# Four stages of a transformer kernel: projections at other steps, fewer unread products, plain down products, folded weights

## The chip, the cores and the metric

The kernel runs on one core of a Trainium2 chip. The time is the device time of one execution in microseconds (us). The engines are TensorE (PE), VectorE (DVE), ScalarE (ACT), GpSimd (POOL) and SyncE (SP, which issues DMAs). PEclk is the clock that TensorE was granted, 1.0 being 2.4 GHz and 0.5 being 1.2 GHz.

## The reference

A sequence batch `x` (64 sequences, 128 tokens, 128 channels) goes through four layers. Layer 0 is window self-attention, top-k cross-attention and a gated MLP. Layers 1 and 2 are each a modulated self-attention with 16 heads of 8 channels, a cross-attention to 77 context rows and a GELU MLP (128 to 512 to 128). Layer 3 ("refine") is a cross-attention with one head to the raw context, whose result goes with the normalised tokens into a router, three experts and a gate. All is float32. What matters here:

```python
# layers 1 and 2, self (cross: q from x, k and v from the context)
x_norm = modulate(_ln(x), shift_a, scale_a)
q, k, v = split(x_norm @ W_qkv + b_qkv)              # 16 heads of 8
x = x + gate_a * (softmax(q @ k.T * scale) @ v @ W_proj + b_proj)
# their MLP
h = gelu(x_norm2 @ W_mlp1 + b_mlp1)
x = x + gate_m * (h @ W_mlp2 + b_mlp2)               # the down product
# layer 3
q, k, v = nx @ Wq, prototype_bank @ Wk, prototype_bank @ Wv
evidence = softmax(q @ k.T * H ** -0.5) @ v
combined = concat([nx, evidence, anchor])            # to router_W, e_w1, gate_w1
```

## The kernel before

The tokens stay in SBUF as `x_res` from the first stage to the last. Work is cut into 16 groups of four sequences (512 tokens). The stages follow one another: setup, window attention, top-k attention, MLP of layer 0 (to 1409 us), attention of layer 1 (to about 2098), its MLP (to 2248), attention of layer 2 (to about 2929), its MLP (to 3084), refine (to the end).

**Attention of layers 1 and 2** (`packed_attention_layer`) takes 32 groups through one pipeline, first 16 of self-attention, then 16 of cross-attention. A group is eight steps, u = 0 to 7 (of half a sequence's heads each). The order on every engine is written out by hand in the `body` functions, and what is done of which group at which step stands in constants:

- At each step PE multiplies queries by keys (`attn_s`, L1616, eight 32-row products), DVE takes row maxima of it (L1491, two), the negated maxima go by ACT (`attn_om`, L1367) and a DMA of POOL back into the packed queries, and seven steps later (LT) PE makes the transposed scores (`attn_t`, L1631), ACT the exponentials (`attn_pT`, L1374, two a step), PE the products with the values (L1656). `s_ps`, the PSUM bank pair of the scores, is single: PE's next scores wait for DVE's maxima, and DVE's next maxima for the scores.
- Two groups ahead, PE transposes the normalised tokens at step XT (L1584), makes keys at KP (L1592), queries at QP (L1597) and values at VP (L1604), all into the one bank `l_ps`. So keys wait until ACT has modulated `attn_hT`; queries until ACT and then DVE have read the keys out of the bank, as a high part (`attn_kT`, L1349) and a low part (L1466); values until the same was done with the queries (`attn_qT`, L1355 and L1471). These are four steps of one chain through PE, ACT and DVE.
- Keys and queries are then packed by DMA (SP: 12 of keys, L1267; 12 of queries, L1253; 2 of zero rows, L1255, a group). SP starts a group's keys when DVE has made their low part and PE has made the last transposed scores of the group before (`s_st`, reached at step 6). ACT's `queries_out` (L1355) waits for the DMAs of the group before, which read the same `attn_qT`.
- The output of a group takes one projection (PROJ, L1756), ACT's `attn_pg` (L1388 to L1392), and is added to `x_res` (L1527).
- `keep_clock` (L1676) issues products that nobody reads, 128x512 each, UNREAD[u] of them at step u, to keep PE busy. They stand behind the step's scores and write `l_ps`.

**The MLPs of layers 1 and 2** (`mlp_layer`) make up and down products as three fp32r products each (`product3`, L238 to L240) from high and low parts, which stand for one fp32 product. The high part of the GELU output `mlp_hid` is a cast of DVE (L1943, four a group), the low part a subtraction of POOL (L1870, three a group) or DVE (L1949, one).

**Refine** takes 16 groups. Per group PE makes keys (L2486), queries (L2491) and values (L2496, eight records), ACT reads out keys (L2385) and queries (L2389), DVE the values (L2246); then scores, softmax, evidence, router, experts.

## Time and profile before

| | |
|---|---|
| median of 3 runs | 3493.57 us (3489.97 to 3500.9) |
| the profiled execution | 3496.01 us, span 3494.2 us |
| PE busy | 3048.8 us, 87% of the span |
| PE weight loads | 2051.7 us |
| DVE | 2754.6 us, 79% |
| ACT | 2253.2 us, 64% |
| POOL | 1170.7 us, 34% |
| PEclk over the run | 0.947 |

The engines' shares are means over stages of different kinds, and none is at 100%, so the stage is what has to be read. Unread products count as busy time of PE. In a row of a timeline the first number is the start in us from the start of the span, the second the busy time of one or more like instructions (xcount); in brackets stands how long the engine had been idle before and what ended the wait.

### The profile page before, as it was taken

The page shows a single profiled execution, that of the slowest core. Times are in us where ns is not written, and L with a number is a line of the kernel's source. Part 1 is how long each engine was busy: PE and PEld are TensorE (multiplying, and loading weights), DVE is VectorE, ACT ScalarE, POOL GpSimd, SP SyncE. Part 2 cuts the span into 40 slices and gives each one's busy share as a digit, 9 for nine tenths or more (in the row PEclk, how much of TensorE's full clock was granted, in tenths as well). Part 3 has the DMA queues.
Part 4 walks back from the last instruction along what each step waited for, and adds up shares of the span by engine and source line. Part 5 has one row for each costly group of instructions (what it writes and reads, how often), then busy time and mean ns, then how long its engine had stood idle before and what let it go on. Part 6 is the DMA issues. An engine that isn't in the chain of part 4 may idle for free. (4 is left out here: it accounts for less than half of the span.)

```text
span 3494.2 us, 94730 instructions
## 1 busy us (share of the span) xinstructions
PE 3048.8 (87%) x32127; PEld 2051.7 (59%) x32127; DVE 2754.6 (79%) x12477; ACT 2253.2 (64%) x5572; POOL 1170.7 (34%) x1374
## 2 busy tenths in 40 slices
PE   6999967777777779799999997789999997879999
PEld 3444434444444457566666665556666665568887
DVE  4878779999999978588877759778887776946665
ACT  2666667777777667377766665457776665646665
POOL 0000046666666656311122215521112212532111
PEclk9999979999899889799999999989999999979999
DMA  1111000000000000244444420034444440000000
GB/s 47 44 49 37 14 12 7 9 9 9 8 9 7 3 1 1 72 106 107 107 103 100 104 60 1 20 97 108 106 107 101 105 100 17 1 24 13 11 12 16
DMA packets 139908, 162.90 MB, mean 47 GB/s; under 512 B 41318, under 2 KB 88870, under 8 KB 139174
## 3 DMA queue, kind: packets, MB, share of 16 engines
q1 hardware_dynamic: 127270, 130.80, 14.9%
q0 software_dynamic: 12160, 26.04, 3.2%
q8 instruction: 262, 4.29, 0.5%
q14 instruction: 216, 1.77, 0.2%
HBM read 16.33 MB, written 4.19 MB: 6 GB/s over the span
## 5 line engine op out<-in xcount | busy, mean ns | idle before, releaser
L1374 ACT ACTIVATE attn_pT<-attn_t 128x512 f32<-128x512 f32 (+1 forms) x1024 | 555.7, 597 | 319.7 <-PE attn_t L1631 319.5
L1491 DVE TENSOR_REDUCE attn_mx<-attn_s 128x4 f32<-128x512 f32 (+1 forms) x1024 | 549.4, 578 | 140.2 <-PE attn_s L1616 139.1
L1616 PEld LDWEIGHTS attn_s<-packed_keys,packed_queries 32*128 32x128 f32 x4096 | 276.7, 189 | 161.5 <-DVE attn_mx L1491 96.0
L659 ACT ACTIVATE topk_prob<-topk_s,topk_nmx 128x77 f32<-128x77 f32 x1024 | 248.3, 326 | 181.7 <-DVE topk_work L840 156.0
L1289 POOL DMA_DIRECT2D packed_queries<-attn_om x256 | 142.7, 557 | 645.0 <-ACT attn_om L1367 640.9
L1616 PE MATMUL attn_s<-packed_keys,packed_queries 32*128 32x128 f32 (+1 forms) x4096 | 341.5, 287 | 13.3 <-DVE attn_mx L1491 7.2
L503 POOL TENSOR_SCALAR topk_mask<-topk_work 128x308 f32<-128x308 f32 x256 | 250.1, 977 | 238.9 <-DVE topk_work L845 237.8
L1023 PE MATMUL topk_s<-kbd,topk_qT 128*128 128x308 f32 x512 | 215.4, 505 | 129.7 <-ACT topk_prob L659 129.2
L1656 PE MATMUL attn_o<-attn_pT,attn_vp 128*18 128x128 f32 (+1 forms) x8192 | 326.3, 277 | 0.0
L1631 PE MATMUL attn_t<-packed_queries,packed_keys 32*128 32x128 f32 (+1 forms) x4096 | 299.8, 264 | 0.0
L1870 POOL TENSOR_TENSOR mlp_hid<-mlp_hid 128x512 fp32r<-128x512 f32 x160 | 210.1, 1314 | 156.8 <-DVE mlp_hid L1943 107.9
L1631 PEld LDWEIGHTS attn_t<-packed_queries,packed_keys 32*128 32x128 f32 (+1 forms) x4096 | 227.4, 166 | 4.7 <-ACT attn_pT L1374 3.4
L1676 PE MATMUL attn_l<-packed_keys 128*128 128x512 f32 x636 | 225.2, 444 | 0.7 <-DVE attn_vp L1481 0.7
L507 POOL TENSOR_TENSOR topk_prob<-topk_prob,topk_mask 128x308 f32<-128x308 f32 x256 | 213.8, 835 | 21.3
L840 DVE MATCH_REPLACE8 topk_work<-topk_top,topk_s 128x77 f32<-128x77 f32 x1024 | 220.2, 223 | 0.0
L1656 PEld LDWEIGHTS attn_o<-attn_pT,attn_vp 128*18 128x18 f32 (+1 forms) x8192 | 181.3, 97 | 60.6 <-issue 44.4
L845 DVE MATCH_REPLACE8 topk_work<-topk_top,topk_work 128x77 f32<-128x77 f32 x1024 | 215.3, 219 | 0.0
L1023 PEld LDWEIGHTS topk_s<-kbd,topk_qT 128*128 128x128 f32 x512 | 86.6, 210 | 195.5 <-ACT topk_prob L659 141.4
L1033 PEld LDWEIGHTS topk_t<-ident,topk_prob 128*77 128x77 f32 x1024 | 146.5, 163 | 58.2 <-issue 16.5
L829 DVE MAX8 topk_top<-topk_s 128x8 f32<-128x77 f32 x1024 | 167.0, 222 | 15.4 <-PE topk_s L1023 15.0
L1033 PE MATMUL topk_t<-ident,topk_prob 128*77 128x128 f32 x1024 | 170.4, 294 | 1.8 <-POOL topk_prob L507 1.8
L1285 POOL TENSOR_TENSOR attn_rstd<-attn_vareps,neg_half 128x4 f32<-128x4 f32 x64 | 65.8, 1029 | 299.9 <-DVE attn_vareps L1449 299.8
(316 smaller groups left out, 7869.7 us busy)
## 6 DMA issues: line engine op xcount, KB each, us to landing
packed_queries<-attn_qT SPq DMA_DIRECT2D x720, 64.0 KB, 2.2
packed_keys<-attn_kT SPq DMA_DIRECT2D x384, 64.0 KB, 2.1
packed_queries<-attn_om POOLq DMA_DIRECT2D x256, 64.0 KB, 2.3
packed_queries<-zero_rows SPq DMA_DIRECT2D x120, 128.0 KB, 2.7
packed_keys<-attn_kT SPq DMA_DIRECT2D x384, 39.0 KB, 2.2
kbd<-window_kT SPq DMA_DIRECT2D x512, 8.0 KB
kbd<-topk_kT SPq DMA_DIRECT2D x512, 4.8 KB
x_res<-in_x SPq DMA_DIRECT2D x16, 192.0 KB, 2.6
```

The lines of the kernel that those rows point to most:

```text
L503: nc.gpsimd.tensor_scalar(mask[:, u % 2, :], work[:, n % NP, :], NEG / 2, None, ALU.is_le).then_inc(s_mask, 1)
L659: last = nc.scalar.activation(prob[:, n % NP, h * keys:(h + 1) * keys], s_ps[:, u % 2, h * keys:(h + 1) * keys], ACT.Exp, scale=SCALE, bia ...
L840: last = nc.vector.match_replace(wk_[now][:, h, :], top[:, u % 2, h, :], sc[:, h, :], NEG)
L845: last = nc.vector.match_replace(wk_[past][:, h, :], top2[:, c % 2, h, :], wk_[past][:, h, :], NEG)
L1023: last = nc.tensor.matmul(s_ps[:, u % 2, 0:cols], qT[:, par, b * T:(b + 1) * T], r.kbd[:, HU * g:HU * g + HU, b * keys:(b + 1) * keys], st ...
L1033: last = nc.tensor.transpose(t_ps[0:rows, c % 2, j * T:(j + 1) * T], prob[:, n % NP, j * rows:(j + 1) * rows], r.ident[:, :])
L1374: nc.scalar.activation(pT[0:keys, c % 2, h, :], t_ps[0:keys, h, :], ACT.Exp, scale=SCALE).then_inc(s_exp, 1)
L1491: nc.vector.tensor_reduce(mx[:, (c // 2) % 2, 2 * k + h, :], sc, AX.X, ALU.max).then_inc(s_max, 1)
L1616: last = nc.tensor.matmul(s_ps[:, h, k * KW:(k + 1) * KW], r.qp[32 * j:32 * j + 32, buf, k, b * T:(b + 1) * T], r.kp[32 * j:32 * j + 32, b ...
L1631: last = nc.tensor.matmul(t_ps[0:keys, h, k * T:(k + 1) * T], r.kp[32 * j:32 * j + 32, buf, k, b * KW:b * KW + keys], r.qp[32 * j:32 * j + ...
L1656: last = nc.tensor.matmul(o_ps[32 * k:32 * k + 18, v * T:(v + 1) * T], vp[0:keys, buf, b, k, v, a, :], pT[0:keys, c % 2, a, k * T:(k + 1) ...
L1676: nc.tensor.matmul(l_ps[:, :], r.kp[:, buf, 0, 0:T], r.kp[:, buf, 0, :], start=True, stop=True)
```

## The change

1. In the attention of layers 1 and 2, XT, KP, QP and VP are 1, 3, 5 and 7 in place of 3, 5, 6 and 7, and the normalisation of the group that comes three later is spread over steps 0, 2, 4 and 6. The unread products are five a group in place of nine, and `keep_clock` stands ahead of the step's scores, behind the wait for the maxima, and writes the scores' bank.
2. In the MLPs of layers 1 and 2 the down product is one plain fp32 product of `hid` and the weights as they are. The casts, the subtractions and the split of the down weights are gone.
3. In refine, a prologue makes `wqk` = Wq times Wk transposed and multiplies Wv into the rows of the experts', the gate's and the router's weights that take the evidence. So the raw context serves as keys and as values: the values are loaded for each group by a DMA of SP into one of three buffers, and the key and value projections and their copies are gone.

```diff
-    XT, KP, QP, VP = 3, 5, 6, 7
+    XT, KP, QP, VP = 1, 3, 5, 7
-    UNREAD = (2, 3, 2, 2)
+    UNREAD = (2, 1, 1, 0, 0, 0, 1, 0)
...
@@ DVE, body
                     if there(before, left, 3):
+                        if u == 0:
+                            ln_stats(i + 3, (0, 1))
                         if u == 2:
-                            ln_stats(i + 3, (0, 1, 2))
-                        if u == 3:
-                            ln_stats(i + 3, (3,))
+                            ln_stats(i + 3, (2, 3))
                             ln_variance(i + 3)
-                        if u == XT + 1:
+                        if u == 4:
                             ln_apply(i + 3, (0, 1))
-                    if u == 0 and i > 0 and there(before, left, 2):
-                        ln_apply(i + 2, (2, 3))
+                        if u == 6:
+                            ln_apply(i + 3, (2, 3))
...
@@ PE
-            def keep_clock(g, buf, count):
-                pe.wait_ge(s_v, min(g + 2, NT))
+            def keep_clock(buf, count):
                 for _ in range(count):
-                    nc.tensor.matmul(l_ps[:, :], r.kp[:, buf, 0, 0:T], r.kp[:, buf, 0, :], start=True, stop=True)
+                    nc.tensor.matmul(s_ps[:, 0, :], r.kp[:, buf, 0, 0:T], r.kp[:, buf, 0, :], start=True, stop=True)
...
                     if now:
                         scores_waits(i, u)
+                        keep_clock(m3, UNREAD[u] if there(before, left, 2) else 2)
...
-                    if now and u < len(UNREAD):
-                        keep_clock(i, m3, UNREAD[u])
...
@@ mlp_layer: DVE loses L1943 and L1949, POOL L1870; PE
+                if not swiglu:
+                    pe.wait_ge(s_hid, n + 1)
+                    nc.tensor.matmul(y_ps[:, par, :], r.W(name, c * C), hid[:, c % NB, :],
+                                     start=(c == 0), stop=(c == NC - 1)).then_inc(s_down, 1)
+                    return
...
@@ refine
+            def load_values(g):
+                sp.dma_start(v[:, g % 3], r.ctx_v[:, G * g:G * g + G, :]).then_inc(s_vin[g % 3], 16)
...
+            nc.tensor.matmul(t_ps[:, 0:C], r.W("q3"), r.W("k3"), start=True, stop=True).then_inc(s_qkps, 1)
...
+                for e in range(E):
+                    out = t_ps[:, e * RH:(e + 1) * RH] if e < 2 else u_ps[:, 1, 2 * C:2 * C + RH]
+                    nc.tensor.matmul(out, r.W("v3"), r.W("e1", (e * 3 + 1) * RH, RH), start=True, stop=True)
+                nc.tensor.matmul(g_ps[:, B * E:B * E + C], r.W("v3"), r.W("g1", C), start=True, stop=True)
+                nc.tensor.matmul(g_ps[:, B * E + C:B * E + C + E], r.W("v3"), r.W("rw", E, E), start=True, stop=True)
...
-                nc.tensor.matmul(l_ps[:, :], r.W("q3"), nx[:, g % NXB, :], start=True, stop=True).then_inc(s_qps, 1)
+                nc.tensor.matmul(l_ps[:, :], wqk[:, :], nx[:, g % NXB, :], start=True, stop=True).then_inc(s_qps, 1)
```

How ACT's work of one self group of layer 1 stands in a row from step 5 on, before (`attn_kT` are the keys, `attn_qT` the queries of two groups ahead, `attn_pT` the exponentials, two a step):

```order
L1374 ACTIVATE attn_pT<-attn_t 128x512 x2
L1349 ACTIVATE attn_kT<-attn_l,bias_cols 128x512
L1392 ACTIVATE attn_pg<-attn_f,gate_bias,mod 128x128
L1367 COPY attn_om<-attn_o 128x384
L1374 ACTIVATE attn_pT<-attn_t 128x512 x2
L1355 ACTIVATE attn_qT<-attn_l,bias_cols 128x512
L1374 ACTIVATE attn_pT<-attn_t 128x512 x2
L1392 ACTIVATE attn_pg<-attn_f,gate_bias,mod 128x128 x3
```

The same engine from step 3 on, now:

```order
L1349 ACTIVATE attn_kT<-attn_l,bias_cols 128x512
L1367 COPY attn_om<-attn_o 128x384
L1374 ACTIVATE attn_pT<-attn_t 128x512 x4
L1355 ACTIVATE attn_qT<-attn_l,bias_cols 128x512
L1392 ACTIVATE attn_pg<-attn_f,gate_bias,mod 128x128
L1367 COPY attn_om<-attn_o 128x384
L1374 ACTIVATE attn_pT<-attn_t 128x512 x4
L1392 ACTIVATE attn_pg<-attn_f,gate_bias,mod 128x128 x3
```

The queries were read out at step 6, behind that step's `attn_pg`, `attn_om` and exponentials; now they stand at step 5 ahead of all of these, and of step 7's exponentials.

PE between the scores of steps 0 and 1, before:

```order
L1681 MATMUL attn_f<-ident,attn_pg 128x128 x4
L1676 MATMUL attn_l<-packed_keys 128x512 x2
L1667 MATMUL attn_r<-ident,attn_om 128x128 x2
L1656 MATMUL attn_o<-attn_pT,attn_vp 18x128 x8
L1616 MATMUL attn_s<-packed_keys,packed_queries 128x128
```

PE at the same place now:

```order
L1680 MATMUL attn_f<-ident,attn_pg 128x128 x4
L1667 MATMUL attn_r<-ident,attn_om 128x128 x2
L1656 MATMUL attn_o<-attn_pT,attn_vp 18x128 x8
L1675 MATMUL attn_s<-packed_keys 128x512
L1616 MATMUL attn_s<-packed_keys,packed_queries 128x128
```

The unread product has moved from a place that needs no maxima to the place between the wait for them and the scores (L1616).

## Rows read from the trace of the kernel before

The columns of a window are its stretch and length, the busy time and the count of instructions of PE, PEld (weight loads), DVE, ACT and POOL (of PE alone in rows 2 and 11, of L1616 and L2008 alone), the granted clock of PE, the busy share of the DMA engines and GB/s.

**Rows 1.** Busy time by engine in three stretches: attention 1, MLP 1, refine.
```profile
1500.00:1750.00 250.00, 234.30 (x3749) 157.96 (x3741) 219.27 (x666) 183.36 (x383) 41.22 (x64) 1.00 0.43 106
2125.00:2225.00 100.00, 82.86 (x378) 59.60 (x377) 92.98 (x248) 64.85 (x141) 58.18 (x47) 1.00 0.00 1
3150.00:3475.00 325.00, 325.00 (x2116) 283.30 (x2115) 205.65 (x615) 200.05 (x542) 66.78 (x54) 1.00 0.05 12
```
**Rows 2.** Windows: scores (L1616) of 11 self groups, 13 cross groups, one cross group.
```profile
1505.45:1728.32 222.87, 58.42 (x705) 1.00 0.44 107
1787.35:2039.08 251.73, 66.90 (x832) 0.99 0.42 103
1963.21:1982.05 18.84, 5.12 (x64) 1.00 0.44 106
```
**Rows 3.** Timeline of PE in one self group of layer 1.
```profile
1568.16 0.32 PE L1616 MATMUL attn_s<-packed_keys,packed_queries 32*128 32x128 f32 x1
1569.36 0.94 PE L1676 MATMUL attn_l<-packed_keys 128*128 128x512 f32 x3
1570.27 0.32 PE L1616 MATMUL attn_s<-packed_keys,packed_queries 32*128 32x128 f32 x1
1577.64 0.32 PE L1616 MATMUL attn_s<-packed_keys,packed_queries 32*128 32x128 f32 x1
1578.92 1.02 PE L1592 MATMUL attn_l<-attn_hT,weights 128*128 128x512 f32 x2
1579.88 0.32 PE L1616 MATMUL attn_s<-packed_keys,packed_queries 32*128 32x128 f32 x1
1581.59 1.13 PE L1597 MATMUL attn_l<-attn_hT,weights 128*128 128x512 f32 x2 [1.05 <-DVE attn_kT L1466]
1585.76 0.29 PE L1616 MATMUL attn_s<-packed_keys,packed_queries 32*128 32x128 f32 x1
```
**Rows 4.** Timeline of DVE in that group, row maxima.
```profile
1568.92 1.29 DVE L1491 TENSOR_REDUCE attn_mx<-attn_s 128x4 f32<-128x512 f32 x2 [0.40 <-PE attn_s L1616]
1581.53 1.28 DVE L1491 TENSOR_REDUCE attn_mx<-attn_s 128x4 f32<-128x512 f32 x2
1584.23 1.28 DVE L1491 TENSOR_REDUCE attn_mx<-attn_s 128x4 f32<-128x512 f32 x2
```
**Rows 5.** Timeline of ACT in that group, the queries' copy.
```profile
1582.84 0.69 ACT L1355 ACTIVATE attn_qT<-attn_l,bias_cols 128x512 fp32r<-128x512 f32 x1 [0.38 <-PE attn_l L1597]
```
**Rows 6.** Timeline of SP: one group's first keys and last zero rows.
```profile
1561.49 8.98 SPq L1267 DMA_DIRECT2D packed_keys<-attn_kT  x12
1579.75 0.64 SPq L1255 DMA_DIRECT2D packed_queries<-zero_rows  x1
```
**Rows 7.** DMA issues of the page: KB each, us from issue to landing.
```profile
packed_queries<-zero_rows SPq DMA_DIRECT2D x120, 128.0 KB, 2.7
```
**Rows 8.** What ACT waited for, 1800 to 2050 us.
```profile
ACT attn_qT L1355 <- DMA packed_queries<-zero_rows: 4.6, 6, 1.4
```
**Rows 9.** Windows of layer 2, before and at a fall of the clock.
```profile
2658.00:2661.40 3.40, 1.52 (x24) 1.12 (x23) 1.58 (x4) 2.02 (x4) 0.00 (x0) 1.00 0.36 93
2661.40:2665.00 3.60, 3.60 (x27) 2.72 (x25) 2.84 (x11) 1.07 (x2) 1.29 (x2) 0.53 0.50 121
```
**Rows 10.** What PE waited for, whole run: us in total, times, longest.
```profile
PE mlp_l L2008 <- DVE mlp_xn L1895: 56.4, 32, 6.3
PE attn_l L1597 <- DVE attn_kT L1466: 54.1, 64, 3.6
```
**Rows 11.** Window of eight MLP groups, their transposes (L2008), four a group.
```profile
2168.05:2237.15 69.10, 5.02 (x32) 1.00 0.00 1
```
**Rows 12.** Timeline of PE in MLP 1: a down product's first record, what follows it.
```profile
2177.90 0.39 PE L238 MATMUL mlp_y<-mlp_hid,mlp_w 128*128 128x512 f32 x1
2178.60 0.60 PE L2048 MATMUL mlp_r<-ident,mlp_pg 128*128 128x128 f32 x4
```
**Rows 13.** Timeline of PE in refine: one group's values.
```profile
3256.66 1.04 PE L2496 MATMUL refine_l<-weights,ctxT 128*77 128x128 f32 x8
```

More of the change, by code:

```diff
@@ L1716, in body @@
                         scores_waits(i, u)
+                        keep_clock(m3, UNREAD[u] if there(before, left, 2) else 2)
+                    elif back:
+                        after(pe, s_max, 2 * NS * NT)
+                        keep_clock((m3 + dg) % 3, 2)
                     if back:
@@ L1731, in body @@
                         rows_of_projection(i - 3)
-                    if now and u < len(UNREAD):
-                        keep_clock(i, m3, UNREAD[u])
-                    elif not there(before, left, 2) and (now or back):
-                        keep_clock(i, m3, 2)
                     if there(before, left, 2):
@@ L1990, in body @@
                     if work and not swiglu:
-                        after(act, s_lo, n - 3)
+                        after(act, s_down, n - 3)
                         act.wait_ge(s_up, n + 1)
@@ L2150, in _ @@
                          ).then_inc(s_rows, 16)
+            for g in range(3):
+                load_values(g)
             for g in range(NG):
                 p = g % 2
+                if there(g + 3):
+                    sp.wait_ge(s_eps, g + 1)
+                    load_values(g + 3)
                 sp.wait_ge(s_y, g + 1)
@@ L2304, in prepared @@
                 nc.vector.tensor_copy(arb[:, :, :], by_batch(g_ps[:, 0:B * E], E)).then_inc(s_arb, 1)
+                for k, (product, parts) in enumerate(folded()):
+                    dve.wait_ge(s_fhi, k + 1)
+                    nc.vector.tensor_tensor(parts[1], product, parts[0].bitcast(F32), ALU.subtract).then_inc(s_flo, 1)
             def gate_bias(g):
@@ L2426, in prepare @@
                 act.wait_ge(s_w3, 16)
[L2427 to L2430 removed]
+                nc.scalar.copy(up_part(0, 0), e1_first).then_inc(s_w1hi, 1)
+                nc.scalar.copy(w1s[:, 0, E * 2 * RH:E * 2 * RH + C], r.W("g1", 0, C)).then_inc(s_w1hi, 1)
             def prepared():
@@ L2438, in prepared @@
                                          ).then_inc(s_w2ow, 1)
+                for k, (product, parts) in enumerate(folded()):
+                    if k == 2:
+                        act.wait_ge(s_arb, 1)
+                        nc.scalar.copy(wr[:, :], g_ps[:, B * E + C:B * E + C + E]).then_inc(s_wr, 1)
+                    nc.scalar.copy(parts[0], product).then_inc(s_fhi, 1)
+            act.wait_ge(s_qkps, 1)
+            nc.scalar.copy(wqk[:, :], t_ps[:, 0:C]).then_inc(s_wqk, 1)
             for i in range(-2, NG):
@@ L2455, in _ @@
                     hidden(i, 3)
-                if new:
-                    keys_out(i + 2)
                 if now:
@@ L2477, in transpose_xn @@
             def transpose_xn(g):
-                after(pe, s_v, g)
+                after(pe, s_qT, g)
                 pe.wait_ge(s_xn, g + 1)
@@ L2614, in _ @@
                     router(i + 1)
-                if new:
-                    project_keys(i + 2)
                 if now:
@@ L2622, in _ @@
                     up(i, 5)
-                if new:
-                    project_values(i + 2)
                 if now:
```

93 lines of the change are left out of this document (41 added, 52 removed).

## The prediction

> **What bounds the kernel now.** I read the page's busy shares first, then windows by stage, because the shares of the whole run mix stages, then the timeline of one group engine by engine, and last the lists of waits. In attention no engine is full: PE is busy 234 of 250 us, but with unread products in that, DVE 219, ACT 183 [rows 1]. What sets the pace is a ring: scores on PE, maxima on DVE, and the next scores. With T for the start of a step's scores and M for its maxima, M comes 0.76 us after T (1568.16 to 1568.92) and the next T 1.35 us after M (1570.27) [rows 3, 4]. Eight such steps would take 17 us; a self group takes 222.87/11 = 20.26 us, a cross group 251.73/13 = 19.36 us [rows 2]. The rest comes from the steps with projections and from DVE's other work. The MLPs are bound by DVE (93 of 100 us, PE 83), refine by PE (325 of 325) [rows 1].
>
> **Attention: a self group step by step.** What the change takes away is the wait of PE's queries for the keys' low part: 64 times, 54.1 us in all [rows 10]. In the group shown it is 1.05 us at 1581.59 [rows 3]. It also removes four of nine unread products; three take 0.91 us from the first to the next scores (1569.36 to 1570.27), so 0.30 each [rows 3]. What it adds: the five that stay stand between the wait for the maxima and the scores, so each of them is on the ring, where the nine stood in gaps. And keys and queries no longer share one stall.
>
> I rebuild a group. T0 is the moment that the maxima of step 7 are done.
> - Steps 0 to 2: two unread products (0.60) and 0.76 to M0; then 1.35 + 0.30 + 0.76 = 2.41 to M1; to M2 the same 2.41, or a little more by DVE, which has in step 1 the maxima (1.29), a normalisation and the addition to x, for which I add 0.03; then 1.35 to T3. Sum 7.56 us.
> - Steps 3 and 4: the keys are projected 1.28 us after T (1577.64 to 1578.92), and their low part comes in front of the next maxima, which start at T + 3.89 (1581.53) [rows 3, 4]. Behind it 1.35: 5.24 us from T3 to T5.
> - Steps 5 and 6: the queries likewise 1.28 after T, the maxima behind their low part 2.64 after that (1581.59 to 1584.23) [rows 3, 4], and one more negation of about 0.08 by my estimate: T + 4.00, + 1.35: 5.35 us from T5 to T7. The unread product of step 6 is covered by this stall.
> - Step 7: 0.76 to M7, and 1.53 from M7 to the next group (1584.23 to 1585.76), which the values' projection sets [rows 3, 4]: 2.29 us.
>
> That is 20.44 us, against 20.26 us on average before [rows 2]. Two stalls of 3.9 and 4.0 us apart cost more than the pair in a row before, and the ring carries 1.2 us of unread products of which the change took no visible time away in the gaps. So the 54.1 us of the removed wait are not won; they turn into DVE waiting at steps 4 and 6.
>
> **The DMAs behind it.** The queries' copy on ACT waits for the DMAs of the group before. SP works from a group's first keys (1561.49) to its last zero rows (1579.75) for 18.26 us, and these land 2.7 us after issue: 20.96 us from the first keys to the landing [rows 6, 7]. Before, the copy that needs it stood at 1582.84, 21.35 us after 1561.49, so 0.4 us to spare [rows 5, 6]; in cross groups, which are shorter, ACT waited there in 6 of about 13, up to 1.4 us [rows 8]. Now the copy stands at step 5, at T5 + 1.28 + 1.25 = T5 + 2.53 (1.25 from 1581.59 to 1582.84 [rows 3, 5]). The keys' DMAs do not start earlier, though the keys are ready two steps sooner: they also wait for the last transposed scores of step 6, about 0.7 us after T6, and T6 is T5 + 0.76 + 1.65 = T5 + 2.41. So the room is the group's length G less (2.41 + 0.7 - 2.53) = G - 0.58, where it was G + 1.28. A late copy by s lengthens the group, and so the room, by s: s = 20.96 + 0.58 - 20.44 - s gives s = 0.55. Self group: 21.0 us, +0.7 on 20.26, times 32: +24 us. What hangs on ACT behind the late copy: `attn_pg`, `attn_om` and the exponentials of steps 6 and 7, for which PE's values and next transposed scores wait.
>
> Cross groups: the one of 18.84 us has no wait for DMAs [rows 2]. By the same steps it becomes about 18.3 (bounds 17.8, if all four removed products and a part of the stall are won, and 18.84, if nothing is). Then s = (20.96 + 0.58 - 18.3)/2 = 1.6: 19.9 us. The rule gives before (20.96 - 1.28 - 18.84)/2 = 0.4, so 19.26 where 19.36 is measured, and I add that 0.1: 20.0, +0.65 on 19.36, times 32: +21 us. Bounds for both kinds together: if landing never binds, self 20.44 and cross 18.3, +6 - 34 = -28 us; if SP's spacing is that of its slower groups, some 21.7 us to the landing, +24 + 21 + 64 x 0.37 = +69.
>
> **The clock.** With fewer unread products and a stall of 1.6 us a cross group PE is idle more. At 2661.4 the granted clock is 0.53 (the 1.2 GHz level) for 3.6 us, and before it PE had been busy for only 1.52 of 3.4 us [rows 9]. Such a fall costs about half its length, 1.7 us. There are four of them in the attention before, all in cross groups; a window of cross groups has 0.99, one of self groups 1.00 [rows 2]. I take 12 more, +20 us; bounds 0 and one in each of 64 groups, +109. The Trainium skill ("TensorE: Matmul & The Clock Gate", section "A second HAM failure mode: psum-queue depth-cycling") says that a PE which is idle in many short bits between groups of matmuls swings between its two clocks. Rows 9 agree that it falls after such a stretch; by that rule most groups would see a fall, which is the slower rival below.
>
> **MLPs.** A group takes 69.10/8 = 8.64 us [rows 11], PE busy 83% [rows 1], so 7.16 us, of which I take 6.8 for work, since records overhang the next ones. DVE loses four casts and a subtraction and is then far from the bound. PE becomes it: the plain fp32 product takes 0.96 us to the next scores (1578.92 to 1579.88) [rows 3], three fp32r products 0.70 (2177.90 to 2178.60) [rows 12]. I keep 0.85 as the lower end, in case the product's start overlaps more here. Four a group add 0.6 to 1.0 to 6.8: 7.6 us. Of 8.64 that saves 1.04, times 16 groups, times 2 layers: -33 us, and 1 for the split in the prologue: -34 (bounds -27, PE at 7.8, and -41). PE's wait for `mlp_xn`, 56.4 us [rows 10], is what it eats into.
>
> **Refine** is PE-bound, so what leaves PE is won: the values (1.04 with the last record's overhang, about 0.8 of PE's time) [rows 13] and the keys (308 of 512 columns of a plain product of 0.96: 0.58) [rows 3]: 1.4 us, times 14 full groups: -20 us. The new prologue puts about eight fp32 products, three copies and three subtractions ahead of the first expert product, partly while the weights' DMA is awaited: +3. Net -17 (bounds -22 and -10). The values' DMAs, 16 of them on SP, which is idle there, are hidden.
>
> **Sum.** +24 + 21 + 20 - 34 - 17 = +14 us on the execution profiled, 3496.0, gives 3510; the median of the runs shown is 3493.6, 2.4 lower: 3508 us.
>
> **Rivals.**
> - A (this forecast, 0.43): DMA landing binds at step 5. 3508, its own range 3480 to 3540.
> - B (0.12), the stall really goes: queries find their keys ready, four products are won in full. Self falls by 54.1/64 = 0.85 and about 0.3 of unread products to 19.1, cross to 18.2: -37 - 37 - 34 - 17 = -125 us, 3369. For it: the wait stands in the list [rows 10]. Against: the chain from projection to DVE's low part is as long at a step of its own.
> - D (0.20), SP and landing do not bind (the DMAs issue faster when they are not behind the keys, or the copy finds them landed): self 20.44, cross 18.3, clock little: -28 - 34 - 17 + 5 = -74 us, 3420. For it: only 6 of 13 cross groups wait today [rows 8].
> - C (0.25), slower: the granted clock falls to 0.5 in most groups, since the wait at step 5 empties PE just where the unread products were taken out. It decides once a stretch like 2658 to 2661.4 comes in every group: half of the groups at 1.7 us, +54, all of them +109, in place of my 20: 3540 to 3600. Against it: three of four steps keep PE near full, and a self group has 20 us of work a group that is 90% busy.
> That the change does not do what it says has no rival here: the order of the engines shows the moves.
>
> **How the numbers follow.** The range, 3425 to 3555, takes in D and the lower half of C and leaves out B and the far end of C, about 2 in 10. No change is within 0.3%, 3483 to 3504, which is about what a measurement of this kernel can tell. A gives slower in 0.25 of its 0.43, same in 0.13, faster in 0.05; C slower, 0.22, with 0.03 same; B and D faster, 0.30, with 0.02 same. So faster 0.35, same 0.18, slower 0.47.
>
> **What would show it.** After the change, ACT's queries' copy waits for the zero rows' DMA in most groups, 0.5 us in self and 1.5 in cross groups; the projection of queries never waits for the keys' low part; self groups take 21.0 and cross groups 20.0 us; maxima at steps 4 and 6 wait for low parts. Each unread product lies right before scores. MLP groups at 7.6 us with PE full; refine's period 1.4 us shorter. Wrong it is if copies do not wait for DMAs (D), if the steps 3 and 5 take 2.3 us (B), or if PEclk shows dips in most groups (C).

## The result, and the profile after

The changed kernel takes 3591.61 us in the median of 4 runs (3560.1 to 3649.82), against 3493.21 us before (3489.97 to 3500.9): the ratio is 1.025 (1.0248), 95% interval 1.017 to 1.033. It is slower, outside of the range on record. The ratios, here and below, leave out runs more than 1.5% above the quickest of their kernel (here 3649.82 us, at a granted clock of 0.894), while the us given are medians of all runs. The execution profiled is the quickest, 3560.1 us with a mean granted clock of 0.926; the two others took 3579 us at 0.915 and 3604 us at 0.910.

From the page of the changed kernel, the span, the busy times and the clock by slices:

```profile
span 3558.3 us, 93096 instructions
PE 3065.5 (86%) x31607; PEld 2017.6 (57%) x31607; DVE 2623.0 (74%) x12300; ACT 2243.9 (63%) x5561; POOL 1044.2 (29%) x1278
...
PEclk9999989999899799899998898989999797989999
```

The busy shares hide the change: PE is at 86%, before at 87%. The stages do, each from PE's first instruction in it to the first of the next: attention 1 went from 691.6 to 750.2 us, attention 2 from 691.0 to 767.6, the two MLPs from 146.1 and 150.2 to 123.7 and 123.7, refine from 405.1 to 384.5. So +135 in attention, -49 in the MLPs, -21 in refine, and 1.6 less before them: 64 us, the difference of the spans.

Windows with the scores alone (L1616), 12 self and 12 cross groups of layer 1, then of layer 2; the columns after the length are PE's busy time in these products, their count, the granted clock, the DMA share and GB/s:

```profile
1509.45:1765.75 256.30, 63.78 (x768) 0.98 0.40 99
1830.45:2089.35 258.90, 64.82 (x768) 0.89 0.38 93
2380.33:2635.14 254.81, 63.73 (x768) 0.98 0.41 101
2703.80:2967.99 264.19, 68.23 (x768) 0.87 0.37 90
```

That is 21.36 and 21.23 us a self group, 21.57 and 22.02 a cross group, where it was 20.26 and 19.36 [rows 2]. The clock is 0.98 in self and 0.89 and 0.87 in cross groups. In the trace's records of the clock there are 33 falls to 0.5 from each layer's group 3 to its group 29 (of 32, counted from 0), 26 of them in cross groups; before there were 4. Together they last 201 us, before 14.

What PE waited for, whole run (us, times, longest), and ACT's copy of the queries:

```profile
PE attn_r L1667 <- ACT attn_om L1367: 95.1, 64, 4.6
PE attn_s L1616 <- DVE attn_mx L1491: 33.8, 67, 1.9
PE mlp_l L2001 <- DVE mlp_xn L1896: 17.9, 4, 6.3
```

```profile
ACT attn_qT L1355 <- DMA packed_queries<-zero_rows: 64.9, 35, 4.4
```

The wait of the queries' projection for the keys' low part, 54.1 us [rows 10], is gone. In its place stands 95.1 us before `attn_r`, the output transposes of step 6. They wait for `attn_om`, ACT's copy, which carries the outputs of an earlier group together with the maxima. The kernel before had this:

```profile
PE attn_r L1667 <- ACT attn_om L1367: 1.7, 4, 0.7
```

ACT in the cross group of layer 1 that is longest delayed, step 6:

```profile
1822.93 0.69 ACT L1355 ACTIVATE attn_qT<-attn_l,bias_cols 128x512 fp32r<-128x512 f32 x1 [3.52 <-DMA packed_queries<-zero_rows]
1823.52 0.45 ACT L1392 ACTIVATE attn_pg<-attn_f,gate_bias,mod 128x128 f32<-128x128 f32 x1
1823.86 0.48 ACT L1367 COPY attn_om<-attn_o 128x384 f32<-128x384 f32 x1
1824.22 1.09 ACT L1374 ACTIVATE attn_pT<-attn_t 77x512 f32<-77x512 f32 x2
```

PE in the same group:

```profile
1818.83 1.02 PE L1597 MATMUL attn_l<-attn_hT,weights 128*128 128x512 f32 x2
1819.29 0.80 PE L1675 MATMUL attn_s<-packed_keys 128*128 128x512 f32 x1
1824.39 0.69 PE L1667 MATMUL attn_r<-ident,attn_om 128*128 128x128 f32 x2 [3.74 <-ACT attn_om L1367]
1828.19 1.89 PE L1604 MATMUL attn_l<-weights,attn_ctxs 128*77 128x128 f32 x8
```

This is the chain that costs. The projection starts at 1818.83, and where nothing else is waited for the copy follows it by 1.2 us, at 1820.0; here it waits until 1822.93 for the last zero rows of the group before to land (ACT is idle for 3.52 us, of which 0.55 are there in every group). `attn_pg`, `attn_om` and the exponentials stand behind it on ACT, PE has nothing to do for 3.74 us before L1667, and then its clock is at half: the values' projection takes 1.89 us for 1.04.

Windows around such a fall in a cross group that did not wait for DMAs, all engines:

```profile
2034.70:2038.10 3.40, 3.40 (x63) 1.96 (x63) 2.38 (x10) 1.61 (x4) 0.23 (x1) 1.00 0.09 24
2038.10:2041.50 3.40, 2.33 (x62) 1.75 (x64) 2.35 (x8) 2.52 (x6) 0.55 (x1) 1.00 0.22 50
2041.50:2044.90 3.40, 3.40 (x29) 2.39 (x21) 2.00 (x8) 1.43 (x3) 0.58 (x1) 0.51 0.28 68
```

The middle one is step 6, with a wait of 1.00 us for `attn_om`: PE is busy 2.33 of 3.40 us, at the full clock. In the next 3.4 us the granted clock is at its 1.2 GHz level. Such a stretch is not always followed by a fall, as e2 shows below.

The MLPs (a window of layer 1) and refine:

```profile
2190.00:2250.00 60.00, 60.00 (x239) 38.61 (x239) 34.76 (x137) 47.01 (x103) 9.37 (x9) 1.00 0.00 1
3250.00:3540.00 290.00, 290.00 (x1885) 253.20 (x1884) 185.53 (x565) 185.78 (x499) 61.88 (x50) 1.00 0.08 19
```

PE of that MLP, two groups' transposes, a down product and what follows it:

```profile
2199.54 0.60 PE L2001 MATMUL mlp_l<-ident,mlp_xn 128*128 128x128 f32 x4
2206.61 0.60 PE L2001 MATMUL mlp_l<-ident,mlp_xn 128*128 128x128 f32 x4
2207.75 1.02 PE L2028 MATMUL mlp_y<-mlp_hid,weights 128*128 128x512 f32 x2
2208.61 0.60 PE L2047 MATMUL mlp_r<-ident,mlp_pg 128*128 128x128 f32 x4
```

PE is at 60 of 60 us, a group takes 7.07 us (2199.54 to 2206.61) for 8.64 [rows 11], and the plain product takes 0.86 us to the next product's start (2207.75 to 2208.61), not 0.96.

### The profile page after: what moved, and what is told of

It reads as the page before. It is cut to its first block and busy times, and to the rows that moved or that the text cites. A ratio compares the mean times of both kernels' runs of the same rounds, so it can differ in the third digit from the quotient of the medians.

```text
span 3558.3 us, 93096 instructions
## 1 busy us (share of the span) xinstructions
PE 3065.5 (86%) x31607; PEld 2017.6 (57%) x31607; DVE 2623.0 (74%) x12300; ACT 2243.9 (63%) x5561; POOL 1044.2 (29%) x1278
## 5 line engine op out<-in xcount | busy, mean ns | idle before, releaser
L1616 PEld LDWEIGHTS attn_s<-packed_keys,packed_queries 32*128 32x128 f32 x4096 | 289.9, 198 | 219.2 <-DVE attn_mx L1491 99.5
L1616 PE MATMUL attn_s<-packed_keys,packed_queries 32*128 32x128 f32 (+1 forms) x4096 | 356.5, 296 | 36.2 <-DVE attn_mx L1491 33.8
L1656 PE MATMUL attn_o<-attn_pT,attn_vp 128*18 128x128 f32 (+1 forms) x8192 | 344.5, 289 | 0.0
L1631 PE MATMUL attn_t<-packed_queries,packed_keys 32*128 32x128 f32 (+1 forms) x4096 | 309.4, 270 | 0.0
L1631 PEld LDWEIGHTS attn_t<-packed_queries,packed_keys 32*128 32x128 f32 (+1 forms) x4096 | 235.4, 172 | 5.5 <-issue 2.9
L1656 PEld LDWEIGHTS attn_o<-attn_pT,attn_vp 128*18 128x18 f32 (+1 forms) x8192 | 187.6, 100 | 65.2 <-issue 45.2
L1675 PE MATMUL attn_s<-packed_keys 128*128 128x512 f32 x392 | 195.1, 545 | 18.6 <-DVE attn_mx L1491 16.5
L1667 PE MATMUL attn_r<-ident,attn_om 128*128 128x128 f32 x512 | 105.5, 289 | 95.1 <-ACT attn_om L1367 95.1
L834 DVE MAX8 topk_top<-topk_work 128x8 f32<-128x77 f32 x1024 | 163.2, 218 | 0.0
```

Of the source, the lines that this page charges most:

```text
L1616: last = nc.tensor.matmul(s_ps[:, h, k * KW:(k + 1) * KW], r.qp[32 * j:32 * j + 32, buf, k, b * T:(b + 1) * T], r.kp[32 * j:32 * j + 32, b ...
L1631: last = nc.tensor.matmul(t_ps[0:keys, h, k * T:(k + 1) * T], r.kp[32 * j:32 * j + 32, buf, k, b * KW:b * KW + keys], r.qp[32 * j:32 * j + ...
L1656: last = nc.tensor.matmul(o_ps[32 * k:32 * k + 18, v * T:(v + 1) * T], vp[0:keys, buf, b, k, v, a, :], pT[0:keys, c % 2, a, k * T:(k + 1) ...
```

## The experiments

Each compares with the kernel before on its own chip; the changed kernel's ratio is 1.0248. "Falls" are counted as above, in the one profiled execution of each kernel. The ring is the circle of scores on PE and maxima on DVE. Names such as e2 are those of the runs, and stand in brackets behind the titles.

**The attention as before, the rest as changed** (e1).

```diff
-    XT, KP, QP, VP = 1, 3, 5, 7
+    XT, KP, QP, VP = 3, 5, 6, 7
...
+    UNREAD = (2, 3, 2, 2)
```

> The changed kernel with the attention of layers 1 and 2 as before; MLPs and refine as changed. Stages of the two traces: MLPs 49.0 us shorter (146.1 to 123.7, 150.2 to 123.7), refine 20.5 shorter (405.1 to 384.5), attention 135.2 longer. Theory 1 (all of the loss is made inside the attention stages, the gains elsewhere are whole): 3493 - 70 = 3423 us. Rival (a part of the loss comes from what the stages do to each other, as a clock that is low at a stage's start): 3440 to 3460.

3431.1 us, ratio 0.9805 (0.9791 to 0.9820): -68 us. The whole loss is made in attention.

**One stage at a time**: the MLPs alone (e10), refine alone (e16), changed in the kernel before.

> The kernel before with the down products of MLPs 1 and 2 as changed, nothing else. Theory 1 (PE becomes the bound of these stages at 7.07 us a group where DVE set 8.64): 16 x 1.57 x 2 = 50 us less, 3493 - 49 = 3444. Rival (the prediction's PE work of 6.8 us and 0.96 per plain product, part of the gain from the stages' ends and the clock there): 34 us less, 3459.

> The kernel before with refine alone as changed. PE is the bound there; per group the values' and the keys' projections go. By the stage's length in the two traces, 405.1 and 384.5 us: 20 us less, 3473. Rival (a part of the 68 us that e1 showed beyond the 40 of the MLPs alone): 28 us less, 3465.

The MLPs alone: 3449.2 us, 0.9890 (0.9873 to 0.9907), -38 us (-44 to -32), its MLP stages 124.2 and 128.4 us long; e1 less refine alone gives -46. The interval takes in the rival's -34 and not the theory's -49; by the stages of the traces it is 44 here and 49 in the changed kernel. So it stays open which of the two sizes holds for the time of the whole kernel. Refine alone: 3469.5 us, 0.9937 (0.9913 to 0.9960), -22 us.

**Two buffers for `attn_qT`** (e2), so that the copy waits for DMAs of two groups before.

```diff
-        qT, kT = sb("qT", [C, 2, GT], F32R), sb("kT", [C, 2, GT], F32R)
+        qT, kT = sb("qT", [C, 2, 2, GT], F32R), sb("kT", [C, 2, GT], F32R)
...
-                    queries_packed(act, g - 1)
+                    queries_packed(act, max(g - 2, 0))
```

> The changed kernel with two buffers for the packed queries' source attn_qT, so that ACT's copy of the queries waits for DMAs of two groups before, not one. Theory 1 (landing of the DMAs binds at step 5 in about every second group): the wait for the zero rows goes, self groups take 20.45 us (what the groups without that wait take now) and cross groups 20.2 us, for 21.3 and 21.8: 32 x 0.85 + 32 x 1.6 = 78 us less, 3482. Rival (the wait is a symptom, PE idles behind attn_om and loses its clock anyway): under 25 us less, 3535 or more.

3449.2 us, 0.9862 (0.9844 to 0.9881): 3.8% less than the changed kernel (0.9862/1.0248). Its windows, as above:

```profile
1507.37:1752.81 245.44, 63.72 (x768) 1.00 0.43 105
1813.01:2044.64 231.63, 63.03 (x768) 0.97 0.42 103
2333.59:2578.69 245.10, 63.67 (x768) 1.00 0.43 105
2638.78:2869.29 230.51, 62.91 (x768) 0.98 0.43 103
```

Self groups are at 20.45 us (all but the last one or two of each window), against 20.44 worked out in the prediction. Cross groups take 18.77 us where the clock stays and 20.24 where it falls once: a fall costs 1.47 us. 11 falls are left. The second buffer took away more than the 78 us expected: 112 us between the two profiled executions, 113 of them in the attention stages. They are the wait and the falls that came with it together; the run does not part them.

One of the cross groups of 18.77 us, at step 6 and behind it, all engines:

```profile
2001.80:2005.20 3.40, 2.33 (x58) 1.75 (x62) 2.27 (x8) 2.52 (x6) 0.55 (x1) 1.00 0.51 121
2005.20:2008.60 3.40, 3.40 (x53) 2.61 (x49) 2.98 (x10) 2.12 (x5) 1.30 (x2) 1.00 0.34 82
```

PE is busy 2.33 of 3.40 us as in the changed kernel, and the clock stays at 1.00. In a cross group with a fall the same stretch (1826.85 to 1830.25) is busy for 2.33 us too, and the clock of the next 3.4 us is 0.51. So the idle stretch is what comes before most falls, but it does not settle alone whether one comes.

**The same wait shortened in another way**: the zero rows' DMAs go from SP to POOL, at step 7 (ZP), with one buffer (e12); and **moved**: queries at step 6, one buffer (e8).

```diff
+                    if u == ZP and there(before, left, 2):
+                        after_alone(pool, s_st, 2 * NS * i)
+                        for gp in range(2):
+                            pool.dma_start(r.qp[3:C:4, (m3 + 2) % 3, 2 * gp:2 * gp + 2, :].bitcast(F32), ...
```

```diff
-    XT, KP, QP, VP = 1, 3, 5, 7
+    XT, KP, QP, VP = 1, 3, 6, 7
```

> The changed kernel (one buffer for attn_qT) with the two DMAs of zero rows a group issued by POOL and not by SP; ACT's copy of the queries does not wait for them, since they do not read attn_qT. This shortens the time from a group's first key DMA to the landing that the copy waits for by two issues of 0.7 us and by 0.6 (2.1 for 2.7 to landing): 20.1 to 18.1 us. Theory 1: the sum of two successive waits is 18.1 + 0.86 - 20.45 in self groups, below zero, and 0.2 in cross groups: the wait goes, 3450 to 3465, as with two buffers. Rival (what binds is the load of the DMA engines, not SP's row of issues): 3540 or more.

> The changed kernel with queries at step 6 again (projections at 1, 3, 6, 7), one buffer. Theory 1 (what binds is the room from a group's first key DMA to the next group's copy of queries): the room grows by a step, 2.4 us, so from G - 0.86 to G + 1.6; landing, 20.1 us after the first key, is then waited for nowhere in self groups and rarely in cross groups. Two queued stalls, queries then values, make the ring a little longer: self 20.7, cross 19.1 us. 3449 + 16 = 3465, clock falls about as in e2. Rival (the stall of the queries' chain at a step of its own is what costs, wherever): 3540 or more.

With POOL: 3503.7 us, 1.0032 (1.0014 to 1.0050), its windows and its wait:

```profile
1504.53:1750.92 246.39, 63.69 (x768) 1.00 0.44 105
1811.27:2067.06 255.79, 68.41 (x768) 0.87 0.39 94
2360.65:2610.90 250.25, 65.07 (x768) 0.98 0.43 103
2675.56:2920.38 244.82, 63.13 (x768) 0.92 0.41 98
```

```profile
ACT attn_qT L1363 <- DMA packed_queries<-attn_qT: 15.2, 12, 3.0
```

So the wait shrinks from 64.9 to 15.2 us and self groups of layer 1 are at 20.5. But 24 falls stay in cross groups. The wait went down nearly as expected, the time did not: 3450 to 3465 was expected, and the 27 falls of this kernel, 136 us at the low clock, were not in that sum. Queries at step 6: 3453.1 us, 0.9884 (0.9855 to 0.9913), 8 falls. ACT's wait:

```profile
ACT attn_qT L1355 <- DMA packed_queries<-zero_rows: 27.5, 22, 2.7
```

It goes down from 64.9 to 27.5 us, and the undisturbed groups are shorter than expected, 20.23 self and 18.12 cross.

**Is it `attn_om` that stands behind the copy on ACT?** The copy behind `attn_om` of step 6, with one buffer (e3) and with two (e6).

```diff
+                    if u == QP + 1 and there(before, left, 2):
+                        queries_out(i + 2)      # behind columns_out, ahead of exponentials
```

> The changed kernel with ACT's copy of the queries at step 6, behind attn_om of that step and ahead of its exponentials; PE's order is as changed. Theory 2 (in cross groups PE idles 1 us before attn_r because attn_om stands behind the queries' copy and attn_pg on ACT, and this idle time makes the granted clock fall in every cross group): the falls go from the cross groups that do not wait for DMAs; cross groups from 20.2 to 18.7 where no DMA is waited for, some 40 us less in all, 3520. Rival (the landing alone matters): no more than 10 us less, 3550.

> The kernel of e2 (two buffers) with ACT's copy of the queries behind attn_om of step 6. In e2 PE idles 1.0 us before attn_r in every cross group and 0.7 in self groups, and 11 clock falls remain. Theory 2a (that idle time is on the path): self 20.45 to 20.2 or less and cross 18.77 to 18.3, falls gone: 20 to 35 us less than e2, 3415 to 3430. Rival (the path runs through the queries' chain, PE to ACT to DVE, which the later copy makes 0.4 us longer; the idle time costs only through the clock): self groups up by 0.3 to 0.4 us, within 10 us of e2, 3440 to 3460.

3590.9 us, 1.0233 (1.0186 to 1.0281) with one buffer, 3475.4 us, 0.9939 (0.9917 to 0.9961) with two, so slower than e2. No gain in either, so the theory falls that this order alone costs the time. It does set PE's wait before `attn_r`, which goes from 49.0 us in e2 to 2.4 in e6. But PE's wait for maxima before the next scores grows from 34.0 to 86.6 us, and e6 has 19 falls where e2 has 11: PE's idle time was moved, not filled.

**More unread products at step 6** (e4), four of them between the scores and the output transposes, one buffer.

```diff
+                        if u == 6 and there(before, left, dg) and there(before, left, 2):
+                            after(pe, s_norm, G * (i + dg) + c // 2)
+                            for _ in range(4):
+                                nc.tensor.matmul(r_ps[:, :], r.kp[:, m3, 0, 0:T], r.kp[:, m3, 0, :], start=True, stop=True)
```

> The changed kernel with four more unread 128x512 products a group at step 6, between the scores and the output transposes, into the rows' bank: PE is busy where it now idles for 1 us. Theory 3 (what costs time in cross groups is the clock, which falls once a group since PE idles at step 6; 1.5 us each): the granted clock stays at 1.0 in the cross groups without a DMA wait, the values' projection takes 1.06 again instead of 1.92 us; 30 to 45 us less, 3515 to 3530. Rival (the clock falls because of the long landing waits, up to 3 us, which four products of 0.27 do not fill): under 10 us less, and 5 to 15 more where the products stand in the way.

3558.8 us, 1.0160 (1.0132 to 1.0188), 16 falls for 33, lasting 171 us for 201. That is 0.9% less than the changed kernel, with intervals that just overlap. ACT's copy still waits up to 4.4 us for DMAs and PE up to 3.7 us before `attn_r`, longer than what four products fill.

**How many unread products, and where.** All with two buffers; e2 has four on the ring (steps 0 to 2) and one at step 6. These have none at all (e7); nine at steps 0 to 3 (e11); only the one of step 6 (e13); only the four (e14).

```diff
-    UNREAD = (2, 1, 1, 0, 0, 0, 1, 0)
+    UNREAD = (0, 0, 0, 0, 0, 0, 0, 0)     # none
+    UNREAD = (2, 3, 2, 2, 0, 0, 0, 0)     # nine
+    UNREAD = (0, 0, 0, 0, 0, 0, 1, 0)     # six
+    UNREAD = (2, 1, 1, 0, 0, 0, 0, 0)     # ring
```

> The kernel of e2 without any unread products inside the groups. Theory 3 (each unread product ahead of the scores is on the ring of scores and maxima): where the clock stays at 1.0, steps 0 to 2 are 0.27 us shorter per product, four of them: self groups 20.45 to 19.4. But with nothing to keep PE busy the clock falls in most groups: 64 x 1.45 = 93 us back; in all 3470 to 3500, with 40 falls or more. Rival (the unread products hardly matter for the clock, its falls came from the landing wait): no more falls than in e2, 11, and 3449 - 60 = 3390.

> The kernel of e2 (two buffers) with nine unread products a group, 2, 3, 2, 2 at steps 0 to 3, all behind the wait for the maxima and ahead of the scores. Theory 3 (every product there is on the ring): e7 has none and 19.64 us, e2 has four on the ring (the one at step 6 is covered) and 20.45: 0.20 each; five more give 21.5 self and 19.8 cross; clock falls go, worth 11 x 1.45: 3449 + 64 x 1.0 - 16 = 3497. Rival (products ahead of the scores fit into gaps as they did behind them): 3430 to 3450.

> The kernel of e2 (two buffers) with one unread product a group, at step 6, and none at steps 0 to 2. Theory 4 (the clock falls at step 7, behind an idle stretch of PE at step 6, and what decides is how busy PE is there): the product at step 6 keeps most groups from falling, as in e2, and the ring is as short as in e7, 19.65 us in self groups and 18.0 in cross groups: 3449 - 64 x 0.8 = 3398. Rival (the unread products of steps 0 to 2 are what keeps the clock): falls as in e7, 29 and some of 20 us, 3480 to 3500.

> The kernel of e2 (two buffers) with the four unread products of steps 0 to 2 and without the one of step 6, the other half of e13. Theory 4: the ring is 20.45 us as in e2, but step 6 has more idle time and falls come in most cross groups and in some self groups, 25 or more: 3449 + 20 to 40 = 3470 to 3490. Rival: as e2, 3445 to 3455, since the product of step 6 is only one of five.

| products at steps 0 to 3, at 6 | ratio (95%) | us | self group without fall | profiled run, us | falls | us at the low clock | PE's wait before `attn_r`, us |
|---|---|---|---|---|---|---|---|
| 4, 1 (e2) | 0.9862 (0.9844 to 0.9881) | 3449.2 | 20.45 | 3447.8 | 11 | 38 | 49.0 |
| 0, 0 (none) | 0.9976 (0.9949 to 1.0002) | 3492.9 | 19.64 | 3512.1 | 29 | 304 | 65.2 |
| 9, 0 (nine) | 1.0486 (1.0455 to 1.0518) | 3659.3 | 21.83 | 3652.3 | 28 | 321 | 63.1 |
| 0, 1 (six) | 0.9934 (0.9879 to 0.9990) | 3499.7 | 19.66 | 3447.9 | 18 | 174 | 49.9 |
| 4, 0 (ring) | 1.0163 (1.0109 to 1.0217) | 3550.2 | 20.46 | 3567.7 | 22 | 341 | 64.7 |

The falls are those of the profiled execution, which for six was the quickest of ten (3447.9 to 3502.7 us) and for none and ring one of the slowest; so the last columns are not those of a median run. Of ring's 341 us, 171 are two falls that begin in group 29 and run on past it.

Windows of layer 1, self and cross, of none, nine, six and ring in this order:

```profile
1503.07:1748.17 245.10, 65.37 (x768) 0.95 0.43 105
1805.47:2072.55 267.08, 76.13 (x768) 0.77 0.37 90
```

```profile
1520.89:1789.77 268.88, 64.19 (x768) 0.97 0.39 96
1850.55:2124.08 273.53, 68.77 (x768) 0.86 0.36 88
```

```profile
1499.08:1739.68 240.60, 64.27 (x768) 0.97 0.44 108
1794.70:2033.72 239.02, 67.13 (x768) 0.89 0.41 101
```

```profile
1504.85:1753.09 248.24, 64.22 (x768) 0.99 0.42 104
1813.04:2085.01 271.97, 73.61 (x768) 0.80 0.36 89
```

A product ahead of the scores costs 0.20 (20.45 - 19.64, four) to 0.28 us (21.83 - 20.45, five more): it is on the ring. For the clock the place matters more than the number. Nine of them, without the one at step 6, have 28 falls; four without it have 22, and the only difference to e2 is that one product. With it, PE's wait before `attn_r` is 49 to 50 us, without it 63 to 65. But the four on the ring count too: six, without them, has 174 us at the low clock for 38 in e2. All but one of the falls in these four kernels start 15.9 us or later in a group, about the end of step 6 or in step 7. My expectation for nine was 160 us too low, that for ring at least 60, and that for six about 100 by the median. For six the rival was right: six is no better than none by time. For none the time was as expected, with fewer and longer falls.

**Step 6 filled**, with two buffers: three products between the scores and the output transposes, and else as in e2 (e15); then without the four on the ring (e17); then with one back at step 0 and one at step 2, behind the scores (e18).

```diff
+                            for _ in range(3):              # at step 6
+                                nc.tensor.matmul(r_ps[:, :], r.kp[:, m3, 0, 0:T], r.kp[:, m3, 0, :], start=True, stop=True)
```

> The kernel of e2 (two buffers) with three more unread products at step 6, between the scores and the output transposes, where PE idles 1.0 us in every cross group. Theory 4: the idle stretch is filled, none or two of the 11 falls are left, and the products cost nothing, being off the ring: 3449 - 14 = 3435. Rival (PE's idle time before attn_r is not what makes the clock fall): falls stay near 11, 3445 to 3455.

3429.5 us, 0.9825 (0.9806 to 0.9844). Its windows, and PE at step 6 of a cross group:

```profile
1506.51:1751.86 245.35, 63.67 (x768) 1.00 0.43 105
1809.02:2034.21 225.19, 61.50 (x768) 1.00 0.43 106
2322.78:2567.84 245.06, 63.69 (x768) 1.00 0.43 105
2624.97:2850.17 225.20, 61.48 (x768) 1.00 0.44 107
```

```profile
2029.41 0.96 PE L1763 MATMUL attn_r<-packed_keys 128*128 128x512 f32 x3
2030.48 0.44 PE L1667 MATMUL attn_r<-ident,attn_om 128*128 128x128 f32 x2
```

Not one fall from group 3 to 29: the clock is 1.00 in all four windows, self groups take 20.45 us (as in e2, all but the last one or two of each window) and cross groups 18.77. The attention stages are 691.4 and 692.2 us long, 1.0 us more than before in all. So the 135 us that attention had lost are the waits and the falls, in sum, and nothing else of the new order. The three products cost the ring nothing; they lie where PE waited 1.01 us for `attn_om` in e2:

```profile
2040.91 0.44 PE L1667 MATMUL attn_r<-ident,attn_om 128*128 128x128 f32 x2 [1.01 <-ACT attn_om L1367]
```

> The kernel of e15 (two buffers, three products filling step 6) without the four unread products of steps 0 to 2. Theories 3 and 4 together: the ring is 0.8 us shorter, self groups 19.65 and cross groups 18.0, and step 6 stays busy, so few falls come: 64 x 0.8 = 50 us under e15, 3379, or some 20 us more with a dozen falls, 3400. Rival (with the ring's products gone other steps are too idle, whatever step 6 does): 25 falls as in e7 and e13, 3450 to 3500.

> The kernel of e17 with one unread product more at step 0 and one at step 2, behind the scores and ahead of the output transposes, so off the ring. Theories 3 and 4: where PE has room between its scores and the end of the maxima they cost nothing, and they keep steps 0 to 2 busy: no falls, self 19.7 and cross 18.1 us: 3380 to 3390. Rival (PE has no room there: scores, values and transposes fill the 2.1 us of a step): each costs up to 0.27 us, so 64 x 0.5 = 35 us over e17.

Without the ring's products 3417.0 us, 0.9766 (0.9743 to 0.9789), 4 falls in the profiled execution, the slowest of six (of 3 to 31 us, three of them early in cross groups), and runs from 3408 to 3451 us. With two back off the ring 3410.2 us, 0.9748 (0.9729 to 0.9767), the lowest of all kernels here, and steady (3408 to 3414 us):

```profile
1503.01:1741.38 238.37, 63.73 (x768) 1.00 0.44 109
1797.12:2029.91 232.79, 64.06 (x768) 0.96 0.43 103
2317.87:2556.22 238.35, 63.70 (x768) 1.00 0.44 108
2612.01:2835.50 223.49, 61.49 (x768) 1.00 0.44 108
```

Self groups 19.86, cross groups 19.40 in layer 1, where one fall of 20.5 us is left, and 18.62 in layer 2. I had expected the two products to cost little or nothing; undisturbed self groups take 19.90 us with them and 19.67 without. e17 lies 17 to 38 us above what I expected of it, e18 20 to 30.

**Candidates.** The attention as before with two buffers (e5), and queries at step 6 with two buffers (e9).

> Attention as before but with two buffers for attn_qT, MLPs and refine as changed (the kernel of e1 and the second buffer). Theory 1 (landing binds only where room is short): before, the copy had 1.28 us of room beyond a group's length, and only about six of 13 cross groups waited, 0.8 us each, with two to five clock falls; so little is left to win: 8 to 15 us under e1, 3417 to 3423. Rival (the second buffer helps whatever the steps, by spreading the DMAs): 30 us or more under e1, 3400.

> The changed kernel with queries at step 6 and two buffers for attn_qT. In e8 (step 6, one buffer) self groups without a disturbance take 20.23 us and cross groups 18.12, the others are longer by DMA waits (11 in 13 cross groups, up to 2.1 us) and clock falls. Theory 1: with the wait gone all groups come near these two: 32 x 0.3 + 32 x 0.9 = 38 us under e8, 3415. Rival (the clock falls stay, since PE has gaps of its own): 3440 to 3450.

3414.1 us, 0.9766 (0.9743 to 0.9790), 3 falls; and 3437.4 us, 0.9862 (0.9838 to 0.9887), 7 falls. The first is as expected. The second is 8 us under e8 by their ratios and not 38, as its rival had it: its cross groups reach 18.12 us, but six of the seven falls are now in self groups, about 15 us into the group. The interval of e5 overlaps that of the best kernel, e18: with the second buffer the new steps are not shown to be worth anything over the old ones.

## Why the prediction was wrong

The direction was right, and the mechanism that it named, the landing of the DMAs, is at work; but the larger part of the loss is another, the clock, which it had put at 20 us. +14 us was forecast; +64 is the profiled execution's, +87 that of the ratio, +98 that of the medians. By its steps:

- *The ring.* Right to 0.01 us in self groups (20.44; 20.45 in e2 and e15), in part by luck. Between the scores' starts of a self group of e2 lie 7.19 us from step 0 to 3, 5.22 to step 5, 5.22 to step 7 and 2.83 to the next group, where the same pieces of the forecast are 6.96, 5.24, 5.35 and 2.89. In cross groups 18.3 was 0.47 too short, which is 15 us over 32 groups: I took four removed products for won, where e15 shows 18.77 against 18.84 before. The price of a product on the ring, 0.30, is 0.20 to 0.28.
- *The landing of the DMAs.* Right in kind: the copy on ACT waits for zero rows, 35 times for 64.9 us, and without the wait (e2) the kernel is 3.8% quicker. The step "a late copy by s lengthens the group, and so the room, by s" fits too, but the lengthening is room for the next group, so that long and short groups often alternate: in layer 1, in a row, 22.83, 20.47, 21.38, 20.47, 23.19 and 20.46 us. The mean of the self groups, 21.3, is near the 21.0 forecast, and the 0.3 more is about what its 7 falls add. From a group's first key to its last zero rows SP took 17.4 us on average (16.4 to 19.5), plus 2.7 to landing: 20.1, less than the 20.96 that I read from one group. SP's first keys start about 0.85 us after step 6 starts, where I had 0.7.
- *The clock.* This is the term that failed: "I take 12 more, +20 us". 29 more came in the profiled execution, with 188 us more at half clock, and in the windows' cross groups there was one in every group. The price was near, 1.47 us for my 1.7; the number and the length of the falls were not. What I had as a rival, C, with 0.25, is what happened, and the time lies in the range given there (3540 to 3600). I argued against it with a mean, PE at 90% in a self group; what counts most is the one stretch at step 6. There the copy on ACT, ahead of `attn_om`, leaves PE 1.0 us idle in cross groups even when no DMA is late, and up to 4.6 when one is. e15 shows it: with no wait for DMAs and the stretch filled the falls are zero. The Trainium skill ("TensorE: Matmul & The Clock Gate", section "A second HAM failure mode: psum-queue depth-cycling") tells of a kernel in which TensorE idles in short bits between groups of matmuls, often enough that its clock swings between the two levels. The changed kernel's trace agrees with it, with a fall in every one of the 24 cross groups of the windows, and I gave it too little weight; e2 agrees only in part, with the same idle bit in its cross groups and falls in 11 of 28.
- *MLPs.* -34 forecast, -49 in the stages of the trace, -38 and -46 by the comparisons. PE's work was 6.43 us a group and not 6.8 (7.07 less four times 0.16, which is 0.86 for the plain product less 0.70), and -49 lies outside of my bounds. My lower end of the product's price was the right one.
- *Refine.* -17 forecast, -21 in the trace, -22 by its own run. Right.
- *The wait removed.* Right that its 54.1 us are not won. I had them turn into DVE's waits at steps 4 and 6, and those steps have the forecast lengths; the 95.1 us that PE waits before `attn_r` I had not foreseen.
- *The range.* The text has it take in D, but D's own number, 3420, lies 5 us below its lower end, 3425.

So +65 for attention was +135, and -51 for the rest was -71 (with the 1.6 us ahead of attention). Ring and landing without the clock had been put at +45: -28 for the ring and +73 for the landing. e15 has +1 for the ring. An estimate parts the rest: the changed kernel has 164 us more at the low clock than e2, which at e2's price (1.47 us for 3.4) are some 70 of the 113 us between them, and leave some 43 for the landing; the clock in all comes to some 90 us, with the 21 between e2 and e15. By that estimate two errors of about 30 us each, in the ring and in the landing, cancelled, and the miss is the clock's. The median of all runs is 31 us above the profiled one, and the clock of the others was lower; that these 31 us are falls too is likely by that, but only one execution has a trace.

What stays open: e12 and e2 have the same order on PE and few waits on ACT, yet 27 and 11 falls (e12 still waits 15.2 us for DMAs, e2 not at all). In both, cross groups of 20.24 us with one fall each follow one another, and in e2 so do groups of 18.77 without; what starts or ends such a row was not tried. Why some falls last 3.4 us and some 14 to 65 is not settled. And no run has e15's three further products at another step, with the one of step 6 kept; that their place does it rests on nine, ring and six.

## What to carry to other kernels

When a wait is taken away by moving an instruction forward, look at everything that now stands behind it in its own engine's queue, and at the other waits of the instruction itself: here a copy moved one step ahead met the DMAs of the group before, and held up the engine that TensorE depends on. A second buffer (4 KB a partition) was worth 3.8% at the new steps and, by e5 against e1, 0.4% at the old ones. And where unread products hold the clock, look at their place before their number: put them into the stretch in which TensorE waits for another engine, and not between a wait and the instruction that ends a ring, where each cost 0.20 to 0.28 us here.

## What the runs showed of the hardware

- One fall of the clock of 3.4 us costs 1.47 us a group (20.24 for 18.77). In the changed kernel's cross groups it comes behind step 6, after a stretch such as 2.33 of 3.40 us busy; in e2 the same stretch is found with a fall behind it and without. Taking out the one 128x512 product at step 6 changed 11 falls to 22 and 3449 us to 3550 (e2, e14).
- Most falls have the granted clock at 0.5 for 3.4 or 6.8 us; others last 14 to 65 us though PE has its usual work (64.9 us in e11, 20.5 in e7 and e13). In e13 a cross group with a fall of 20.5 us takes 25.4 us, where its neighbour takes 18.9.
- A plain fp32 product of 128x512 takes 0.86 us to the start of the next product (2207.75 to 2208.61 in the changed kernel), three fp32r products 0.70 [rows 12].
